# Copying the half tile's weights on the sync engine, one quarter in each of four rounds

## The chip, the cores and the metric

The kernel runs on one core of one Trainium2 chip. The metric is the device time of one execution in microseconds. The engines are PE (TensorE, matrix products), DVE (VectorE), ACT (ScalarE), POOL (GpSimd) and SP (SyncE, which here only issues DMAs). A difference of over 0.3% (about 1.1 us) is what a measurement of this kernel can tell from none.

## What is computed

A gated block: a LayerNorm and a cross-attention of 2048 tokens (8 sequences of 256, width 256) over 77 context rows each, then a LayerNorm and a feed-forward part. The feed-forward part has a shared expert for all tokens and two routed experts, each token going to one of them. Cut to what matters:

```
def ffn(x):                                   # x: 2048 tokens, width 256
    top1 = argmax(softmax(x @ gate_w.T))      # 0 or 1 for each token
    masked = x[None] * one_hot(top1).T[:, :, None]
    h = relu(einsum('end,edh->enh', masked, w1) + b1[:, None])    # hidden width 1024
    routed = (einsum('enh,ehd->end', h, w2) + b2[:, None]).sum(0)
    return routed + relu(x @ sw1 + sb1) @ sw2 + sb2

x = x + tanh(g_xattn) * xattn(layernorm(x), ctx)
x = x + tanh(g_ffn) * ffn(layernorm(x))
```

For the expert that a token is not sent to, the masked row is zero, so that expert gives a constant row, relu(b1) @ w2, which the kernel works out once from its weights (the tile `other_sum`).

## The kernel before

Every matrix product runs on float32 data that is cut into a high and a low part (`_hi`, `_lo`), in three products: high by high, high by low, low by high. ACT makes the high part out of a PSUM bank, DVE or GpSimd subtracts it to get the low part. So each step of PE has one of ACT and one of DVE (or GpSimd) behind it before PE can use the result.

**The first stage** (0 to about 226 us) holds the attention of eight batches and the shared expert's feed-forward part in five units. Its order is written out by hand, an order for each engine (`PE_ORDER`, `ACT_ORDER`, `DVE_ORDER`, `POOL_ORDER`, `SP_ORDER`); a word such as `tn.5.0.1` is a step, its indices and, last, which of two PSUM banks (`bank`) it uses. The steps that matter here:
- `sc.b.k` on PE: scores of batch b, quarter k; then `sm` and `ss` on DVE (maxima L1246, the shift L1258), `ex` on ACT, `su` on DVE (sums L1264 and reciprocals L1268), `di` on GpSimd (the division L678);
- `tn` transposes of the probabilities (L1668), `va` the product with the values and `val` its low part on DVE (L1273), `ou` the output product, `x1` the addition to x (L1282);
- `xn2` on ACT (L964) and `n2` on PE (L1705): second LayerNorm and its transposes; `h` and `y`: the shared expert's two products; `hl` (L1379) the low part of h;
- `ot.e.part` on DVE (L1228, L1232): half of the sums over `w2` for `other_sum` of expert e, four instructions each; `ch` (L1302 and on): which expert a token goes to; `scat` on GpSimd: the scatter of the tokens' rows into `sorted_dram`, sorted by expert.

**The seam.** When the last counts are there, DVE writes a plan of five integers to SBUF (`plan_int`): how many tiles of 256 sorted rows belong to the first expert (`first`), how many rounds there are (`rounds`, eight on this data), whether a tile is taken twice, and place and expert of a half tile that both experts share. Each engine loads those that it needs into registers with `value_load` (L576 to L579 on SP, L782 and L783 on GpSimd, L1062 to L1064 on ACT, L1462 and L1463 on DVE). SP does that after it has issued the store of the last unit of the shared part (L545, `ps.4`), which waits for DVE's addition (L1388).

**The routed stage** is a loop of eight rounds on every engine. Round j multiplies one tile of 256 sorted rows with one expert's weights, which lie in SBUF in `ew`. PE makes eight chunks of h (four banks, so three run ahead), from the fourth on a chunk of y after each (L1535), and behind the seventh chunk of h, ahead of the fourth of y, it transposes the tile of the round to come, `sorted_turn(j + 1)`, L1772; for that the tile must have been loaded into `xs`. SP loads it (L549) once the tile before has been transposed and once DVE has copied that one's token numbers (`ids_copied`, L1475), which DVE does right after its first low part of the round:

```
with sp.Fori(0, rounds - 1) as j:
    sp.wait_ge(xsT_ps, j + 1)
    sp.wait_ge(ids_copied, j + 1)
    load_sorted(j + 1 - again)
```

GpSimd gathers the rows of `part_dram` (what the shared expert gave) with two indirect DMAs (L795), adds the constant row (L802), waits for DVE's `final` (L1488, which takes y and part), and scatters it to `out` (L808).

**The half tile** comes last (from about 331 us). Its expert is known at the seam only, so its weights are copied from `ew` over the shared expert's, which are free when the shared part is done. ACT issues those four copies of 1 MB each, before its loop (L1071, L1074); PE waits for them with `half_w` just before the half tile:

```
act.wait_ge(y_used, CHUNKS_SHARED)
for n in range(2, 6):
    act.wait_ge(w_lo[n], 1)
for n in range(2):
    act.dma_start(sw1_sb[n]..., ew[:, bass.ds(half_expert, 1), n, :]...).then_inc(half_w, 16)
    act.dma_start(sw2_sb[n]..., ew[:, bass.ds(half_expert, 1), 2 + n, :]...).then_inc(half_w, 16)
```

## Time and profile before

| | |
|---|---|
| three runs | 352.29, 352.46, 353.43 us; median 352.46 |
| the profiled execution's own time | 350.86 us |
| its span | 349.1 us |
| PE busy | 319.1 us (91% of the span) |
| DVE, ACT, POOL busy | 230.1, 216.4, 184.4 us |
| TensorE's granted clock, mean | 0.974 of full |
| moved by DMA | 35.69 MB |

The span is the time from the first to the last instruction that the profile holds; the execution's own time has 1.8 us more around it. The profile gives the busy time of each engine in all, and in stretches; which wait ended an engine's idle time; and a chain of waits, followed back from the last instruction. Times of instructions are counted from the span's start. The granted clock is 1.00 at 2.4 GHz and 0.50 at 1.2 GHz.

### The profile page before, as it was taken

How to read it: one execution, taken by the hardware profiler on the slowest of the kernel's cores; microseconds unless marked ns; L12 is line 12 of the kernel's file. 1: busy time of each engine (PE TensorE's matmuls, PEld its weight loads, DVE VectorE, ACT ScalarE, POOL GpSimd, SP SyncE). 2: the span in 40 equal slices, each digit the busy share in tenths (PEclk: the TensorE clock that was granted, in tenths of full speed). 3: DMA queues.
4: the chain of work that ended last, by engine and by line, in shares of the span. 5: the costliest groups of instructions: out<-in, count | busy, mean ns of one | idle time of the engine just before them, and what ended most of it. 6: DMA issues, size and time to landing. Idle time of an engine off the chain costs nothing.

```text
span 349.1 us, 7274 instructions
## 1 busy us (share of the span) xinstructions
PE 319.1 (91%) x2363; PEld 284.6 (82%) x2363; DVE 230.1 (66%) x516; ACT 216.4 (62%) x483; POOL 184.4 (53%) x261
## 2 busy tenths in 40 slices
PE   7996688999989999999999999964999999999980
PEld 7764557779878788887998899964999999999970
DVE  6999789899989878877847936321344454445370
ACT  2765998869577577579764854442447554755560
POOL 8317989893643485736530775303245434563441
PEclk9999899999999999999999999988999999999995
DMA  6991846636131040431421004095023212321310
GB/s 192 297 327 31 257 103 157 141 95 207 16 94 38 5 118 0 107 105 48 168 74 60 0 17 141 29 366 207 4 86 90 67 25 88 92 60 30 91 46 12
DMA packets 38151, 35.69 MB, mean 102 GB/s; under 512 B 16608, under 2 KB 35060, under 8 KB 37613
## 3 DMA queue, kind: packets, MB, share of 16 engines
q1 hardware_dynamic: 33992, 23.17, 24.2%
q0 software_dynamic: 2720, 7.32, 6.4%
q10 hardware_dynamic: 1413, 4.87, 3.8%
q8 instruction: 14, 0.23, 0.3%
q14 instruction: 12, 0.10, 0.1%
HBM read 21.20 MB, written 9.85 MB: 89 GB/s over the span
## 4 chain that ended last, share of the span: by engine, by line
PE 68%; DVE 11%; DMA 7%; ACT 6%; issue 3%; SPq 2%; POOL 0%; ACTq 0%; DVEq 0%; POOLq 0%
PE y_ps L1535 25%; PE h_ps L1535 18%; PE bank L1535 10%; PE s_ps L1535 9%; DMA x_all<-in_x 5%; PE bank L1668 4%; DMA xs<-sorted_dram 3%; DVE rsum L1264 1%; PE bank L1772 1%; DVE stats L1147 1%; DVE probs L1258 1%; ACT xn L885 1%; DVE smax L1246 1%; PE bank L1705 1%; ACT pT L943 1%
## 5 line engine op out<-in xcount | busy, mean ns | idle before, releaser
L678 POOL TENSOR_TENSOR probs<-probs,rinv 128x616 f32<-128x616 f32 x32 | 41.3, 1294 | 37.2 <-DVE rinv L1268 36.9
L1469 DVE TENSOR_TENSOR hT_lo<-h,hT_hi 128x256 fp32r<-128x256 f32 x64 | 29.6, 463 | 43.4 <-ACT h L1086 43.4
L1535 PE MATMUL y_ps<-ew,hT_hi 128*128 128x256 f32 x256 | 54.3, 290 | 3.0 <-DVE hT_lo L1469 3.0
L1535 PEld LDWEIGHTS y_ps<-ew,hT_hi 128*128 128x128 f32 x256 | 43.4, 194 | 3.2 <-DVE hT_lo L1469 3.2
L1535 PE MATMUL y_ps<-sw_hi,hT_hi 128*128 128x256 f32 x136 | 40.7, 299 | 1.2 <-DVE hT_lo L1513 1.2
L982 ACT ACTIVATE hT_hi<-h_ps,vec_cols 128x512 fp32r<-128x512 f32 (+1 forms) x40 | 24.3, 608 | 24.0 <-PE h_ps L1535 23.6
L1535 PE MATMUL y_ps<-sw_lo,hT_hi 128*128 128x256 f32 x136 | 38.4, 282 | 0.0
L1535 PE MATMUL y_ps<-sw_hi,hT_lo 128*128 128x256 f32 x136 | 38.4, 282 | 0.0
L1083 ACT ACTIVATE hT_hi<-h_ps,vec_cols 128x256 fp32r<-128x256 f32 x32 | 15.2, 475 | 35.1 <-PE h_ps L1535 28.5
L1535 PE MATMUL y_ps<-ew,hT_lo 128*128 128x256 f32 x128 | 36.6, 286 | 0.0
L808 POOL DMA_INDIRECT out<-final,scatter_token x16 | 18.1, 1129 | 30.2 <-issue 30.2
L1264 DVE TENSOR_REDUCE rsum<-probs 128x8 f32<-128x616 f32 x32 | 25.1, 786 | 9.7 <-ACT probs L934 4.8
L1535 PE MATMUL h_ps<-x2T_hi,sw_hi 128*128 128x512 f32 (+1 forms) x80 | 29.7, 371 | 0.0
L704 POOL TENSOR_TENSOR hT_lo<-h,hT_hi 128x512 fp32r<-128x512 f32 (+1 forms) x15 | 17.3, 1156 | 23.0 <-ACT h L987 22.8
L1535 PEld LDWEIGHTS y_ps<-sw_hi,hT_hi 128*128 128x128 f32 x136 | 25.9, 191 | 2.8 <-DVE hT_lo L1513 1.8
L1535 PE MATMUL h_ps<-x2T_hi,sw_lo 128*128 128x512 f32 (+1 forms) x80 | 27.9, 349 | 0.0
L1535 PE MATMUL h_ps<-x2T_lo,sw_hi 128*128 128x512 f32 (+1 forms) x80 | 27.8, 348 | 0.0
L943 ACT ACTIVATE pT<-bank 128x512 f32<-128x512 f32 x40 | 23.4, 604 | 6.8 <-PE bank L1668 6.6
L1379 DVE TENSOR_TENSOR hT_lo<-h,hT_hi 128x512 fp32r<-128x512 f32 (+1 forms) x25 | 17.5, 701 | 15.3 <-ACT h L987 15.2
L1535 PE MATMUL h_ps<-xsT_parts,ew 128*128 x192 | 27.0, 284 | 0.0
L1535 PE MATMUL s_ps<-xsT_parts,ew 128*128 x192 | 26.9, 283 | 0.0
L1535 PEld LDWEIGHTS y_ps<-sw_hi,hT_lo 128*128 128x128 f32 x136 | 25.9, 191 | 0.2
(214 smaller groups left out, 920.1 us busy)
## 6 DMA issues: line engine op xcount, KB each, us to landing
v_diag<-v_rows SPq DMA_DIRECT2D x16, 256.0 KB
stage<-in_L_ffn_w SPq DMA_DIRECT2D x4, 1024.0 KB, 5.7
xs<-sorted_dram SPq DMA_DIRECT2D x8, 257.0 KB
stage<-in_L_ffn_sw SPq DMA_DIRECT2D x2, 1024.0 KB, 6.7
sw_hi<-ew ACTq DMA_DIRECT2D x2, 1024.0 KB, 5.9
sw_lo<-ew ACTq DMA_DIRECT2D x2, 1024.0 KB, 10.2
x_all<-in_x SPq DMA_DIRECT2D x1, 1536.0 KB, 10.1
part_dram<-x_all SPq DMA_DIRECT2D x3, 512.0 KB, 2.9
```

What stands on the lines that cost most here:

```text
L678: nc.gpsimd.tensor_tensor(pq, pq, rinv[:, b % 2, k, :].unsqueeze(2).to_broadcast([P, HG, KEYS]), ALU.mult).then_inc(p_ready, 1)
L704: nc.gpsimd.tensor_tensor(hT[1][:, q % HB, 0:width], h32[:, q % 2, 0:width], hT[0][:, q % HB, 0:width], ALU.subtract).then_inc(h_lo_pool, 1)
L808: pool.indirect_dma_start(out=out[:, :], out_offset=bass.IndirectOffsetOnAxis(ap=scatter_token[:, t:t + 1], axis=0), in_=final[:, t, :], i ...
L885: ins = nc.scalar.activation(xn[:, b % 2, t, :], x_all[:, n, :], ACT.Identity, scale=rstd[:, n:n + 1], bias=shift[:, n:n + 1])
L943: nc.scalar.activation(pT[:, 2 * u:2 * u + 2, :].rearrange("p c s -> p (c s)"), bank[m][:, :], ACT.Copy).then_inc(pT_sb, 1)
L982: nc.scalar.activation(hT[0][:, q % HB, 0:width], h_ps[:, q % 2, 0:width], ACT.Relu, bias=b1_sb[:, 0, c:c + 1]).then_inc(h_hi, 1)
L1083: nc.scalar.activation(hT[0][:, c % HB, 0:RTOK], hidden_bank(c % 4)[:, 0:RTOK], ACT.Relu, bias=b1_sb[:, 1 + e, c:c + 1]).then_inc(h_hi, 1)
L1264: nc.vector.tensor_reduce(out=rsum[:, b % 2, k, :], in_=probs[:, b % 2, k, :].rearrange("p (h k) -> p h k", k=KEYS), axis=AX_X, op=ALU.add ...
L1379: nc.vector.tensor_tensor(hT[1][:, q % HB, 0:width], h32[:, q % 2, 0:width], hT[0][:, q % HB, 0:width], ALU.subtract).then_inc(h_lo, 1)
L1469: nc.vector.tensor_tensor(hT[1][:, c % HB, 0:RTOK], h32[:, c % 2, 0:RTOK], hT[0][:, c % HB, 0:RTOK], ALU.subtract).then_inc(h_lo, 1)
L1535: return nc.tensor.matmul(out_, lhsT, rhs, start=start, stop=stop, **kw)
L1668: ins = nc.tensor.transpose(bank[m][0:ROWS[c], v * SEQ + t * P:v * SEQ + (t + 1) * P], probs[:, b % 2, g * TB + t, ROW0[c]:ROW0[c] + ROWS[ ...
```

## The change

There are four edits.

1. ACT no longer issues the four copies, and no longer loads `half_expert`. SP issues them, one in each of its rounds 0 to 3, right behind that round's load of a tile, on the same queue. So that a register can choose the quarter, the shared expert's four weight tiles become one tile `sw` with an index of four.
2. SP waits once for the experts' low parts (`w_lo`) ahead of its loop, and its loop is cut in two, rounds 0 to 3 and the rest.
3. GpSimd drains once in every round (`pool.drain()`), behind its two additions and ahead of its wait for `final_rdy`.
4. The written orders of the first stage change. Up to the middle of the stage only DVE, ACT and GpSimd differ; from batch 5 on many steps use the other of the two banks (the routed stage too: `SORTED_BANK` 0), and a few steps change places. Two of the lines that show it, the second a cut row of `PE_ORDER`:

```
-SORTED_BANK = 1
+SORTED_BANK = 0
-    y.1.2 sc.6.1 tn.5.0.1 ou.4.0 h.1.6 tn.5.1.1 y.1.3 sc.6.2 h.1.7 tn.5.2.0
+    y.1.2 tn.5.0.0 ou.4.1 h.1.6 sc.6.1 tn.5.1.0 y.1.3 h.1.7 tn.5.2.1 sc.6.2
```

The rest of the diff:

```
-        sw1_sb = [sb(f"sw1_{n}", [P, KC, HIDDEN], F32R) for n in ("hi", "lo")]
-        sw2_sb = [sb(f"sw2_{n}", [P, HC, DIM], F32R) for n in ("hi", "lo")]
+        sw = sb("sw", [P, 4, KC * HIDDEN], F32R)
+        sw1_sb = [sw[:, n, :].rearrange("p (k h) -> p k h", k=KC) for n in range(2)]
+        sw2_sb = [sw[:, 2 + n, :].rearrange("p (k d) -> p k d", k=HC) for n in range(2)]
...
-            with sp.Fori(0, rounds - 1) as j:
+            def routed(j):
                 sp.wait_ge(xsT_ps, j + 1)
                 sp.wait_ge(ids_copied, j + 1)
                 load_sorted(j + 1 - again)
+
+
+            for n in range(2, 6):
+                sp.wait_ge(w_lo[n], 1)
+            with sp.Fori(0, 4) as j:
+                routed(j)
+                sp.wait_ge(y_used, CHUNKS_SHARED)
+                sp.dma_start(sw[:, bass.ds(j, 1), :].rearrange("p o h -> p (o h)").bitcast(F32),
+                             ew[:, bass.ds(half_expert, 1), bass.ds(j, 1), :].rearrange("p e o h -> p (e o h)").bitcast(F32)
+                             ).then_inc(half_w, 16)
+            with sp.Fori(4, rounds - 1) as j:
+                routed(j)
...
                     nc.gpsimd.tensor_tensor(part[:, t, :], part[:, t, :], other_row[:, 1 - e, :], ALU.add
                                             ).then_inc(part_rdy, 1)
+                pool.drain()
                 pool.wait_ge(seam_rdy, 1)
...
-            half_expert = act.value_load(plan_int[0:1, HALF_EXPERT:HALF_EXPERT + 1], min_val=0, max_val=1)
-
-
-            act.wait_ge(y_used, CHUNKS_SHARED)
-            for n in range(2, 6):
-                act.wait_ge(w_lo[n], 1)
-            for n in range(2):
-                act.dma_start(sw1_sb[n][:, :, :].rearrange("p k h -> p (k h)").bitcast(F32),
-                              ew[:, bass.ds(half_expert, 1), n, :].rearrange("p o h -> p (o h)").bitcast(F32)
-                              ).then_inc(half_w, 16)
-                act.dma_start(sw2_sb[n][:, :, :].rearrange("p k d -> p (k d)").bitcast(F32),
-                              ew[:, bass.ds(half_expert, 1), 2 + n, :].rearrange("p o h -> p (o h)").bitcast(F32)
-                              ).then_inc(half_w, 16)
```

**SP at the head of the routed loop** (`xs<-sorted_dram` is a tile's load, `sw<-ew` a copy of 1 MB, `ISA` a register operation that carries waits). Before:

```order
L579 ISA x2
L581 UNCONDITIONAL_BRANCH
L581 ISA
L549 ISA
L549 DMA xs<-sorted_dram 128x2x257
L581 ISA
L581 COMPARE_AND_BRANCH
```

and now (from L589 on the changed kernel's line numbers):

```order
L579 ISA x2
L589 UNCONDITIONAL_BRANCH
L589 ISA
L549 ISA
L549 DMA xs<-sorted_dram 128x2x257
L592 ISA
L592 REGISTER_ALU
L592 DMA sw<-ew 128x2048
L589 REGISTER_ALU
L589 COMPARE_AND_BRANCH
```

The load keeps its place as the first DMA of SP's loop, and the copy stands behind it.

**ACT at the head of the routed loop.** Before:

```order
L1064 TENSOR_LOAD plan_int
L1064 ISA x2
L1071 ISA
L1071 DMA sw_hi<-ew 128x2048
L1074 ISA
L1074 DMA sw_hi<-ew 128x2048
L1071 ISA
L1071 DMA sw_lo<-ew 128x2048
L1074 ISA
L1074 DMA sw_lo<-ew 128x2048
L1095 UNCONDITIONAL_BRANCH
```

and now (its L1076 is the L1063 of before):

```order
L1076 TENSOR_LOAD plan_int
L1076 ISA x2
L1095 UNCONDITIONAL_BRANCH
L1095 ISA
L1082 REGISTER_ALU
L1083 ACTIVATE hT_hi<-h_ps,vec_cols 128x256
```

The loop's first ACTIVATE now comes right behind the two register loads.

**DVE around the shift of batch 5's last scores** (`ss.5.3` is the first L1258 here). Before:

```order
L1258 TENSOR_TENSOR probs<-s_ps,smax 128x616
L1273 TENSOR_TENSOR oT_lo<-bank,oT_hi 128x512
L1264 TENSOR_REDUCE rsum<-probs 128x8
L1268 RECIPROCAL rinv<-rsum 128x8
L1246 TENSOR_REDUCE smax<-s_ps 128x8
L1258 TENSOR_TENSOR probs<-s_ps,smax 128x616
```

and now:

```order
L1258 TENSOR_TENSOR probs<-s_ps,smax 128x616
L1228 TENSOR_SCALAR other_sum<-stage,relu_b 128x256
L1232 SCALAR_TENSOR_TENSOR other_sum<-stage,relu_b,other_sum 128x256 x3
L1273 TENSOR_TENSOR oT_lo<-bank,oT_hi 128x512
L1232 SCALAR_TENSOR_TENSOR other_sum<-stage,relu_b,other_sum 128x256 x4
L1264 TENSOR_REDUCE rsum<-probs 128x8
L1268 RECIPROCAL rinv<-rsum 128x8
```

The eight instructions of `ot.0.0` and `ot.0.1` stood some 45 us earlier, between 79 and 93 us of the profile, and stand here now.

## Rows read from the trace of the kernel before

**Rows 1.** Busy time by stretch: stretch and its length, engines, clock, DMA share, GB/s
```profile
120.00:160.00 40.00, 40.00 (x295) 33.89 (x292) 31.66 (x79) 26.36 (x61) 25.85 (x36) 1.00 0.28 80
220.00:240.00 20.00, 15.23 (x113) 14.70 (x111) 6.17 (x13) 8.45 (x21) 4.80 (x6) 0.91 0.62 238
240.00:260.00 20.00, 17.30 (x135) 17.30 (x136) 6.66 (x14) 8.32 (x20) 7.30 (x8) 0.91 0.18 52
280.00:300.00 20.00, 20.00 (x172) 20.00 (x171) 9.57 (x21) 11.77 (x30) 9.15 (x10) 1.00 0.20 48
```

**Rows 2.** The chain of waits, 226 to 262 us: start, length, what
```profile
226.44 0.76 DVE x_all L1388
...
227.69 1.09 SPq L576
...
233.08 9.58 DMA xs<-sorted_dram
...
251.90 0.71 PE y_ps L1535 x6
...
256.13 0.44 PE bank L1772 x4
```

**Rows 3.** The timeline around the first round: start, length, instruction, idle before it
```profile
226.53 0.57 ACTq L1071 DMA_DIRECT2D sw_hi<-ew  x1
...
230.85 0.47 ACT L1083 ACTIVATE hT_hi<-h_ps,vec_cols 128x256 fp32r<-128x256 f32 x1 [6.57 <-issue]
...
232.20 0.48 PE L1535 MATMUL y_ps<-ew,hT_hi 128*128 128x256 f32 x1 [2.99 <-DVE hT_lo L1469]
...
242.70 1.11 PE L1772 MATMUL bank<-ident,xs 128*128 128x128 f32 x4 [4.48 <-DMA xs<-sorted_dram]
```

**Rows 4.** Busy time in three short stretches, columns as in rows 1
```profile
233.00:234.00 1.00, 1.00 (x7) 1.00 (x7) 0.52 (x2) 0.88 (x3) 0.00 (x0) 0.50 1.05 434
240.00:241.00 1.00, 0.00 (x0) 0.00 (x0) 0.00 (x0) 0.00 (x0) 0.00 (x0) 1.00 0.64 240
242.70:246.00 3.30, 3.30 (x16) 3.30 (x17) 0.69 (x1) 0.60 (x1) 1.41 (x2) 0.50 0.00 0
```

**Rows 5.** DMA from 216.9 to 223 us in 40 slices, and SP's issue
```profile
GB/s 369 329 363 282 67 0 27 161 88 135 243 310 351 250 148 41 7 7 20 20 27 0 0 0 0 0 0 0 0 0 0 0 0 0 0 0 0 0 0 0
...
216.92 0.37 SPq L549 DMA_DIRECT2D xs<-sorted_dram  x1
```

**Rows 6.** The timeline of PE: two transposes that it waited for
```profile
98.84 0.63 PE L1705 MATMUL bank<-ident,xn 128*128 128x128 f32 x4 [0.75 <-ACT xn L964]
...
100.59 0.66 PE L1705 MATMUL bank<-ident,xn 128*128 128x128 f32 x4 [0.41 <-DVE oT_lo L1273]
```

**Rows 7.** The timeline of DVE: the sums that move, and a wait near their new place
```profile
79.19 0.35 DVE L1228 TENSOR_SCALAR other_sum<-stage,relu_b 128x256 f32<-128x256 f32 x1
79.58 1.89 DVE L1232 SCALAR_TENSOR_TENSOR other_sum<-stage,relu_b,other_sum 128x256 f32<-128x256 f32 x3
...
90.64 2.04 DVE L1232 SCALAR_TENSOR_TENSOR other_sum<-stage,relu_b,other_sum 128x256 f32<-128x256 f32 x4
...
128.30 0.79 DVE L1264 TENSOR_REDUCE rsum<-probs 128x8 f32<-128x616 f32 x1 [1.55 <-ACT probs L924]
```

**Rows 8.** The timeline of GpSimd, and DVE's two sums of a round
```profile
235.88 1.07 POOL L795 DMA_INDIRECT part<-part_dram,gather_token  x1 [11.73 <-issue]
...
243.32 1.41 POOL L802 TENSOR_TENSOR part<-part,other_row 128x256 f32<-128x256 f32 x2 [5.07 <-DMA part<-part_dram,gather_token]
...
253.85 1.04 POOL L795 DMA_INDIRECT part<-part_dram,gather_token  x1 [0.30 <-issue]
...
258.09 1.43 POOL L802 TENSOR_TENSOR part<-part,other_row 128x256 f32<-128x256 f32 x2 [1.87 <-DMA part<-part_dram,gather_token]
...
249.29 0.75 DVE L1488 SCALAR_TENSOR_TENSOR final<-y_ps,gains,part 128x512 f32<-128x512 f32 x1 [1.69 <-PE y_ps L1535]
...
261.03 0.75 DVE L1488 SCALAR_TENSOR_TENSOR final<-y_ps,gains,part 128x512 f32<-128x512 f32 x1 [1.23 <-PE y_ps L1535]
```

53 lines of the change are left out of this document (26 added, 27 removed).

## The prediction

> **What bounds the kernel now.** I read three views, in this order. The busy time by stretch shows where PE rests: over 120 to 160 us and over 280 to 300 us it is busy throughout, so the late first stage and the steady rounds are PE's, but of 220 to 240 us it works 15.23, and of 240 to 260 us 17.30, at a clock of 0.91 [rows 1]. That is the step from the first stage into the routed one. The chain of waits says what these 7.5 us wait for: DVE's last addition of the shared part, then SP, which from 227.69 us on loads its four registers at about 1.1 us each, then one DMA, the load of tile 1, from 233.08 to 242.66 us, then PE's transposes at 242.70, which waited 4.48 us for it [rows 2, 3]. The timeline gives the rest: ACT issues four copies from 226.53 us on and starts the routed part only at 230.85, after 6.57 us; PE gets its first low part at 232.20, after 2.99 us of idle time [rows 3]. After both rests the clock stands at 0.50: in the stretch at 233 us and in that from 242.70 us on [rows 4].
>
> The load takes 9.58 us because it shares the DMA engines with 4 MB of copies: at 233 us they are fully busy (share 1.05, 434 GB/s), and only at 240 us does that fall to 0.64 [rows 4]. The same instruction for tile 0 was issued at 216.92 us, with no copy beside it, and the last bytes move in the 21st slice of 0.1525 us, so within 3.2 us [rows 5].
>
> **Part by part.**
>
> *ACT issues nothing.* PE has its four banks of h filled at 229.21 (232.20 less 2.99 [rows 3]); at 0.71 us a chunk [rows 2] the first was there at about 227.1, and ACT can start then. DVE has its own two register loads to do behind the addition that ends at 227.20; at SP's 1.09 us each [rows 2] it is ready by 229.4 at the latest. So PE's first y starts at 229.2 to 229.9 instead of 232.20, and the 2.99 us go. But what is late next is the load: PE's work from the first y to the transposes is 4.23 us in the next round (251.90 to 256.13 [rows 2]), so it stands at the transposes at 233.4 to 234.1 and waits there. Worth nothing by itself: the load hides it.
>
> *The load without copies beside it.* SP's own chain does not get shorter; the four waits on `w_lo` were fulfilled long ago and cost a few hundredths each (estimate: 0.1 us, from the pieces around the load that are not 1 us long). Issue at 233.2, 3.1 us for the transfer (the last slices of rows 5 carry next to nothing, and PE needs the completion), so 236.3 us instead of 242.66: **6.4 us** less. Bounds on the transfer: not under 2.5 us (the bulk in rows 5 is over after 16 slices), not over some 4.6 us (in the round after, SP may issue the load only once the first low part is made, PE's first y begins right behind that at 251.90, and PE transposes at 256.13 without waiting [rows 2]).
>
> *The copies.* Each goes behind its round's load on SP's queue, is 1 MB, and takes about 3.3 us of all engines (four of them, from about 227.5 to 240.6 us [rows 3, 4]) in a round of 11.74 us (249.29 to 261.03 [rows 8]). The next load is issued a round later, so it finds the queue empty. PE needs the copies only behind its eighth round; the last is issued in round 3. The gathers of `part` do meet the copy: alone they take 4.24 us from the first issue to the additions (253.85 to 258.09), among the four copies 7.44 (235.88 to 243.32 [rows 8]). With one copy, which began before them, I expect about 1 us more, and the cover is this: the additions end at 259.52, `final` waits for PE until 261.03, so 1.2 us are free in each round (with 0.3 us between them), and PE needs `final` only with the first y of the next round, 1.9 us after it ends (250.04 to 251.90). Cost 0.
>
> *The drain.* It stands behind additions that are over at 259.52 and ahead of a wait that ends at 261.78. The trace has no drain on GpSimd that I could read; it costs between 0 and, as a bound from the nearest GpSimd instructions, the 1.43 us of the two additions [rows 8]. I take what is left of their running time, which is hidden: 0. Uncovered it would delay only the scatter.
>
> *The orders of the first stage.* The eight `ot` instructions leave DVE's stretch from 79 to 93 us, 0.35 + 1.89 + 2.04 us [rows 7]. Behind that stretch PE waits twice, 0.75 us for ACT's `xn2` and 0.41 us for DVE's low part [rows 6]; `xn2` now stands ahead of one shared chunk on ACT, and DVE is earlier. At most 1.16 us go; I take **0.8**. At 123 us the same 4.3 us come in ahead of and behind `val.4`; DVE has 1.55 us of idle time before 128.30 [rows 7], and `sc.6.1` and `sc.6.2` on PE, which wait for the scores before them to be read, were moved behind other steps of PE (a transpose, an output product and an h chunk; an h chunk and a transpose), which is what such a lateness needs. I take 0 there. The changed banks are the same work in the other bank.
>
> *The clock.* PE will still rest 2.2 to 2.8 us before the transposes (236.3 less 233.4 to 234.1). Both rests at the seam, 2.99 and 4.48 us [rows 3], were followed by a stretch at 0.50, the second by 3.3 us of it on the path (242.70 to 246.00 [rows 4]). I expect one again: 0. If none comes, half of 3.3 us, 1.6 us, is gained.
>
> The sum: 6.4 + 0.8 = 7.2 us. The profiled execution took 350.86 us (span 349.1), so it would take 343.7; it lies 1.6 us below the median of the three runs, 352.46, to which the same is applied: **345.3 us**.
>
> One rule of the Trainium skill speaks against the plain reading. "DMA: Bandwidth & Descriptors", section "Issuing engines are not separate DMA queues", says that DMAs of any engine run on the same 16 DMA engines and interleave, and that spreading the issue saves only sequencer time. The trace agrees on the sharing; on the sequencer it shows 6.57 us of idle ACT for four issues and two register loads, which is not small. By that rule alone the copy behind the load would still eat into it; that is the first rival.
>
> **The rivals.**
>
> 1. *The copy slows its own load.* The copy can be issued some 0.4 us after the load (the issue's own 0.37 us [rows 5]), which needs 3.1 us. If they share the engines evenly, the load ends up to one copy later, 3.3 us. For it: the load of tile 1 was slowed by exactly such copies. Against: there they were on another queue and ahead. It would also reach into rounds 1 to 3, where the load has 4.6 us at most. Time: 345.3 + 3.3 = 348.6.
> 2. *DVE is late at 123 us.* The 4.3 us of sums against 1.55 us idle: 2.7 us stand on PE's path if the moved score steps do not cover them, and PE has no rest of its own there (120 to 160 us [rows 1]). Time: 348.0.
> 3. *GpSimd's loop becomes the bound, and the kernel slower.* If each gather among copies takes 3.2 us more, as in round 0 (7.44 less 4.24), four rounds are 2.0 us late each, less 1.9 us of PE's slack: 6.1 us. A drain of length X delays the scatter by X less 1.05 us (the time in which `final` is made) in each of them. Above X = 1.3 us the gain is gone; at 2.4 us (as long as both scatters' issues) it is 6.1 + 4 x 1.35 + 4 x 0.15 = 12.1 us against 7.2: 357.4. Against: the adds are 1.4 us in all, and only one copy is there at a time.
> 4. *The load is slow by itself* in the loop's first round and the copies only lie beside it. Then only 0.8 us go: 351.7. Rows 5 speak against it.
>
> **How the numbers follow.** Forecast 0.79, rivals 0.08, 0.07, 0.04, 0.02. The range: at the low end the clock's 1.6 us and the rest of the 1.16 us, 343.3, rounded to 343.0 for the transfer's lower bound; at the high end the first rival, 348.5. Faster by over 0.3% (under 351.4; about what a measurement can tell): forecast and rivals 1 and 2, 0.94; within it rival 4, 0.02; slower rival 3, 0.04.
>
> **What would show it.** The chain of waits should hold SP's register loads, then the load of about 3 us and the transposes near 236; ACT's first routed ACTIVATE near 227.1; no idle PE before the first y, or under 0.8 us; PE waiting 2 to 3 us for `xs` once, then 0.50 for 3.4 us. PE's waits at 98.8 and 100.6 should be gone or smaller, and none new between 122 and 137. Rounds of 11.74 us throughout, the additions of rounds 0 to 3 up to 1 us later. I am wrong if the load takes over 4.6 us, if PE waits for `final`, or if DVE's last addition of the shared part starts later than at 226.44.

## The result, and the profile after

| | before | changed |
|---|---|---|
| runs | 351.59 to 353.43 us, median 352.38 (4) | 339.61 to 343.43 us, median 340.71 (4) |
| the profiled execution | 350.86 us, span 349.1 | 340.90 us, span 339.1 |
| PE busy | 319.1 us | 318.2 us |
| TensorE's granted clock, mean | 0.974 | 0.980 |

The ratio is 0.9679 with a 95% interval of 0.9616 to 0.9741. The medians lie 11.7 us apart, and the interval stands for 9.1 to 13.5 us. The forecast was 7.1 us faster (345.3 us), its range ended at 343.0. The direction was right and the size was not: 4.6 us more came than was forecast.

The busy time by stretch of the changed kernel, beside [rows 1] (same columns):

```profile
120.00:160.00 40.00, 38.69 (x286) 32.41 (x283) 34.76 (x83) 24.31 (x54) 25.15 (x35) 1.00 0.28 80
220.00:240.00 20.00, 19.63 (x165) 19.29 (x164) 7.66 (x16) 10.48 (x26) 5.26 (x6) 1.00 0.33 106
240.00:260.00 20.00, 19.39 (x160) 18.77 (x159) 7.75 (x19) 10.97 (x27) 11.34 (x12) 1.00 0.45 150
280.00:300.00 20.00, 20.00 (x172) 20.00 (x171) 8.86 (x21) 12.11 (x31) 11.30 (x12) 1.00 0.27 79
```

PE works 19.63 us of 220 to 240 us, where it was 15.23, and the clock is full at the seam, where it was 0.91. Between 120 and 160 us it now has 1.3 us of gaps that it did not have.

The timeline of the changed kernel around the first round (start, length, instruction, idle before it), beside [rows 3]:

```profile
227.57 0.75 DVE L1388 SCALAR_TENSOR_TENSOR x_all<-y_ps,gains,x_all 128x512 f32<-128x512 f32 x1 [1.07 <-PE y_ps L1535]
228.36 0.48 ACT L1083 ACTIVATE hT_hi<-h_ps,vec_cols 128x256 fp32r<-128x256 f32 x1 [2.96 <-PE h_ps L1535]
232.01 0.42 SPq L549 DMA_DIRECT2D xs<-sorted_dram  x1
232.78 0.63 SPq L592 DMA_DIRECT2D sw<-ew  x1
234.93 0.66 PE L1772 MATMUL bank<-ident,xs 128*128 128x128 f32 x4 [0.37 <-DMA xs<-sorted_dram]
```

ACT starts the routed part 0.79 us behind the start of DVE's addition (it was 4.41), the load is issued 4.44 us behind it (it was 6.64), and PE waits 0.37 us for `xs` where it waited 4.48. PE has no wait of its own before its first y. The last two rows put a bound on the load: issued at 232.01 and used at 234.93, at most 2.9 us, where the forecast had 3.1 and the kernel before 9.58 [rows 2].

SP's four register loads, by source line (duration in ns min/median/max, then the start), which I had priced at 1.09 us each whatever happens:

```profile
L576 SPq TENSOR_LOAD <-plan_int x1: 607/607/607, 228.8 to 228.8; - x1
L577 SPq TENSOR_LOAD <-plan_int x1: 282/282/282, 229.8 to 229.8; - x1
L578 SPq TENSOR_LOAD <-plan_int x1: 262/262/262, 230.3 to 230.3; - x1
L579 SPq TENSOR_LOAD <-plan_int x1: 273/273/273, 230.9 to 230.9; - x1
```

Together they take 1.42 us, where the chain of before has 1.09 us for the first alone [rows 2] and the four together take 3.77.

The end of the program, which I had not read at all: GpSimd's last instruction but for its semaphores is a drain, the instruction that the third edit adds to every round. This one belongs to the end of the block (L177). Before and after:

```profile
L177 POOLq DRAIN  x1: 4650/4650/4650, 344.2 to 344.2; - x1
```

```profile
L177 POOLq DRAIN  x1: 375/375/375, 338.5 to 338.5; - x1
```

And DVE's last sum of the loop and that of the half tile (L1488, L1528), in the timelines of before and of the changed kernel:

```profile
331.57 0.75 DVE L1488 SCALAR_TENSOR_TENSOR final<-y_ps,gains,part 128x512 f32<-128x512 f32 x1 [1.53 <-PE y_ps L1535]
340.34 0.48 DVE L1528 SCALAR_TENSOR_TENSOR half_final<-y_ps,gains,half_part 128x256 f32<-128x256 f32 x1 [0.80 <-PE y_ps L1535]
```

```profile
325.78 0.75 DVE L1488 SCALAR_TENSOR_TENSOR final<-y_ps,gains,part 128x512 f32<-128x512 f32 x1 [1.24 <-PE y_ps L1535]
334.60 0.48 DVE L1528 SCALAR_TENSOR_TENSOR half_final<-y_ps,gains,half_part 128x256 f32<-128x256 f32 x1 [0.80 <-PE y_ps L1535]
```

With these milestones the 10.0 us between the two spans can be laid out, each line the difference of two starts:

| stretch | before | changed | less |
|---|---|---|---|
| start to DVE's last shared addition | 226.44 | 227.57 | -1.13 |
| from there to the first transposes of the loop (242.70, 234.93) | 16.26 | 7.36 | 8.90 |
| to the first `final` (249.29, 241.86) | 6.59 | 6.93 | -0.34 |
| to the eighth `final` (331.57, 325.78) | 82.28 | 83.92 | -1.64 |
| to the half tile's (340.34, 334.60) | 8.77 | 8.82 | -0.05 |
| to the end of the span | 8.8 | 4.5 | 4.3 |

So the seam gave 8.9 us, the end 4.3, and 3.2 us were given back, in the first stage and in the rounds. The profiled execution of before lies 1.5 us under its median, that of the changed kernel 0.2 us over its own; the rest of the 11.7 us is in that. Two theories had to be told apart for each: for the end, that the drains in the rounds shorten it (A) or that something in the copies' move does (B); for the seam, that the bytes of the copies slow three different things (register loads, ACT's own issues, the load), or that the issues as such do.

### The profile page after: what moved, and what is told of

Its sections match the earlier page's. It is cut to its first block, busy times and chain, and to the rows that moved or that the text cites. A ratio compares the mean times of both kernels' runs of the same rounds, so it can differ in the third digit from the quotient of the medians.

```text
span 339.1 us, 7286 instructions
## 1 busy us (share of the span) xinstructions
PE 318.2 (94%) x2363; PEld 282.2 (83%) x2363; DVE 227.9 (67%) x516; ACT 215.6 (64%) x483; POOL 184.0 (54%) x261
## 4 chain that ended last, share of the span: by engine, by line
PE 61%; DVE 15%; ACT 8%; issue 7%; DMA 5%; POOL 1%; POOLq 1%; SPq 1%; DVEq 0%; ACTq 0%
PE y_ps L1535 20%; PE h_ps L1535 17%; PE bank L1535 9%; PE s_ps L1535 9%; DMA x_all<-in_x 5%; PE bank L1668 4%; ACT probs L947 2%; DVE rsum L1264 2%; DVE smax L1246 1%; DVE probs L1258 1%; DVE stats L1147 1%; DVE other_sum L1232 1%; ACT pT L956 1%; DVE hT_lo L1469 1%; ACT xn L898 1%
## 5 line engine op out<-in xcount | busy, mean ns | idle before, releaser
L690 POOL TENSOR_TENSOR probs<-probs,rinv 128x616 f32<-128x616 f32 x32 | 39.1, 1223 | 37.8 <-DVE rinv L1268 37.5
L1535 PE MATMUL y_ps<-sw,hT_hi 128*128 128x256 f32 x272 | 57.1, 290 | 1.2 <-DVE hT_lo L1513 1.2
L1535 PEld LDWEIGHTS y_ps<-sw,hT_hi 128*128 128x128 f32 x272 | 44.9, 191 | 2.9 <-DVE hT_lo L1513 1.8
L1535 PE MATMUL h_ps<-x2T_hi,sw 128*128 128x512 f32 (+1 forms) x160 | 43.6, 359 | 0.1
L1535 PE MATMUL y_ps<-sw,hT_lo 128*128 128x256 f32 x136 | 38.4, 282 | 0.0
L1535 PEld LDWEIGHTS h_ps<-x2T_hi,sw 128*128 128x128 f32 x160 | 26.8, 190 | 3.5 <-issue 0.8
L1535 PE MATMUL h_ps<-x2T_lo,sw 128*128 128x512 f32 (+1 forms) x80 | 27.8, 348 | 0.0
L1379 DVE TENSOR_TENSOR hT_lo<-h,hT_hi 128x512 fp32r<-128x512 f32 (+1 forms) x25 | 16.2, 654 | 15.0 <-ACT h L1000 15.0
L1535 PEld LDWEIGHTS y_ps<-sw,hT_lo 128*128 128x128 f32 x136 | 26.0, 191 | 0.2
L1668 PE MATMUL bank<-ident,probs 128*128 128x128 f32 (+1 forms) x160 | 24.3, 284 | 1.4 <-ACT pT L956 1.0
```

The costliest lines, as they stand in the source:

```text
L690: nc.gpsimd.tensor_tensor(pq, pq, rinv[:, b % 2, k, :].unsqueeze(2).to_broadcast([P, HG, KEYS]), ALU.mult).then_inc(p_ready, 1)
L1379: nc.vector.tensor_tensor(hT[1][:, q % HB, 0:width], h32[:, q % 2, 0:width], hT[0][:, q % HB, 0:width], ALU.subtract).then_inc(h_lo, 1)
L1535: return nc.tensor.matmul(out_, lhsT, rhs, start=start, stop=stop, **kw)
L1668: ins = nc.tensor.transpose(bank[m][0:ROWS[c], v * SEQ + t * P:v * SEQ + (t + 1) * P], probs[:, b % 2, g * TB + t, ROW0[c]:ROW0[c] + ROWS[ ...
```

## The experiments

Each kernel was timed beside the kernel before on the same chip (its own runs and those of before stand beside each other; the chips differ by some us, so medians are compared within a row or a table only). The intervals are 0.4 to 0.6% wide to each side, so what is under 2 us is read from the traces and not from the times. Diffs are cut to what changes.

### Which part of the change gives what: e1, e2, e3, e5

The changed kernel without the drain (e1), and the kernel before with the drain (e2):

```
-                pool.drain()
                 pool.wait_ge(seam_rdy, 1)
```

```
                                             ).then_inc(part_rdy, 1)
+                pool.drain()
                 pool.wait_ge(seam_rdy, 1)
```

> The changed kernel without GpSimd's drain in the rounds; all else as changed. Theory A (the trace of the changed kernel): the drain that GpSimd makes at the very end of the program took 4.65 us before and 0.38 us now, because the drains in the rounds have left it nothing to do, so the tail grows again by 4.3 us: 345.0 us. If the drains are also what makes three rounds longer (periods of 12.1 to 12.6 us among 11.75), that comes back and it is 342.6 us with periods of 11.75. Theory B (the drain does nothing, the end is shorter since the copies left ACT's queue): 340.7 us, tail unchanged. The prediction's own price, 0, says 340.7 us too.

> The kernel before with the drain in each round as the one edit. Theory A: the seam stays, the tail loses 4.3 us: 352.4 - 4.3 = 348.1 us; if the drains lengthen some rounds by 0.8 us, up to 350.5. Theory B and the prediction's price of 0: 352.4 us, with about 9.2 us between PE's last product and the end as before.

e3 is the changed kernel without the drain and with `SORTED_BANK` and all written orders of before; e5 is the kernel before with `SORTED_BANK` and all written orders of the change:

> The copies on SP, a quarter in each of rounds 0 to 3, with the orders of before and no drain. The prediction's term: 6.4 us, so 346.0 us, with register loads on SP of 1 us each and PE resting 2 to 3 us before the transposes. Theory A: the register loads were slowed by the copies too and take 0.3 us each, PE rests under 1 us, both stretches at half clock go: 2.99 + 4.48 + 3.3 = 10.8 us, so 341.6 us; with rounds lengthened by the copies 344.0 us. Theory B (the tail too comes from this edit): 337.3 us.

> The new orders and banks alone in the kernel before. The prediction's term: 0.8 us less, 351.6 us, with DVE's last shared addition at 225.6. Reading of the two traces: PE's waits at 98.8 and 100.6 us go (1.9 us less at 105 us), and new ones come between 122 and 150 us (1.5 to 2 us): 352.0 to 352.7 us. If the bank of the routed stage's transposes lengthens rounds (ACT late by 1.5 us once a round): 354 to 355 us.

| kernel | median (range) | before beside it | ratio (95%) |
|---|---|---|---|
| e1, changed without drain | 344.52 (342.81 to 347.93) | 349.77 | 0.9854 (0.9799 to 0.9910) |
| e2, drain alone | 345.35 (342.70 to 346.42) | 349.77 | 0.9855 (0.9806 to 0.9904) |
| e3, copies on SP alone | 346.19 (343.87 to 347.65) | 349.77 | 0.9872 (0.9822 to 0.9921) |
| e5, orders alone | 350.23 (347.52 to 352.34) | 349.77 | 1.0014 (0.9973 to 1.0054) |

The drain by itself gives 4.4 us by the medians (3.4 to 6.8 by the interval), as theory A said (4.3). The last drain of the program, in e1 and in e2:

```profile
L177 POOLq DRAIN  x1: 4650/4650/4650, 336.2 to 336.2; - x1
```

```profile
L177 POOLq DRAIN  x1: 375/375/375, 340.4 to 340.4; - x1
```

Theory B falls: e1 has the copies on SP and its end takes 4.65 us all the same. e2's rounds stayed between 11.72 and 11.94 us, so drains do not lengthen them. The orders by themselves give nothing that can be measured; my 0.8 us (a ratio of 0.998) lies inside the interval, and so does 0. e3 gave 3.6 us, less than any of the numbers that stood ready for it (6.4, 8.4 and 10.8). In its trace the seam is as short as in the changed kernel, the shared addition at 229.82 us and the transposes at 236.92, so 7.10 us; but the addition came 3.4 us later than in the kernel before, and its rounds took 83.7 us where those of before took 82.3. With six runs over 3.8 us, and the interval up to 0.9921, how much this edit is worth alone stays open between 2.8 and 6.2 us. e1, which has it and the orders, gave 5.25 (3.1 to 7.0).

The traces of this chip say why that is less than the 8.9 us of the first pair. Two of them have the copies on ACT, e2 and e5, and from the shared addition to the transposes they take 14.42 and 14.70 us, not 16.26, since PE rests only 1.35 and 2.83 us for `xs`. The seam of e1 and e3 (7.16 and 7.10) is then 7.4 us shorter. And the first two turns of the loop, from the first transposes to the third, take 25.99 and 26.21 us in e1 and e3, and 23.55 and 23.56 in e2 and e5. What is left is about 5 us, which is e1's gain and lies within e3's interval.

### Both kernels again on one chip, and the shape of the copies: e6 to e9

> The kernel before once more, profiled on the chip that runs the next three. If the load of tile 1 took 9.6 us because of the four copies alone, it takes 9.6 again, and PE rests 4.5 us at the transposes. In the kernels with parts of the change that left the copies on ACT (the drain alone, the orders alone) it took 7.7 and 8.0 us and PE rested 1.35 and 2.83 us: if that is how much one execution differs from another, this trace shows 7.5 to 9.6 us, and the seam of the first trace was a slow one. ACT's stalls of 1.0 to 1.5 us ahead of one ACTIVATE a round, which the first trace lacked and the other five have: present here too if they belong to single executions, absent if the edits bring them.

> The changed kernel once more on the same chip. If the parts add up (on the other chip: drain alone -4.4 us, copies alone -3.6, the drain taken from the whole +4 from the sum of what is left), it is 8 to 10 us faster than before here; if the 11.7 us of the first comparison hold everywhere, 11.7.

e8 takes the drain out of the rounds and puts one behind the loop:

```
                 routed(j, 1)
 
+            pool.drain()
             pool.wait_ge(half_ids, 1)
```

> The changed kernel with one drain of GpSimd behind its loop, ahead of the half tile, in place of one a round. Theory A, form 1 (the drain at the end works off what has piled up since the last drain): the one drain takes some 4 us, beside the half tile's wait, where GpSimd has about 3 us to spare ahead of its gather; the drain at the end is 0.4 us, and the time that of the changed kernel to +1 us. Form 2 (the drain at the end is long if any DMA of GpSimd was issued since the last one): in the changed kernel there are four such DMAs behind the last drain and it took 0.38 us, so form 2 is already unlikely; it would give +4.3 us here and there alike.

e9 issues all four copies behind the first load of the loop:

```
-            with sp.Fori(0, 4) as j:
+            with sp.Fori(0, 1) as j:
                 routed(j)
-                sp.wait_ge(y_used, CHUNKS_SHARED)
-                sp.dma_start(sw[:, bass.ds(j, 1), :]..., ew[:, bass.ds(half_expert, 1), bass.ds(j, 1), :]...)
-            with sp.Fori(4, rounds - 1) as j:
+            sp.wait_ge(y_used, CHUNKS_SHARED)
+            for n in range(4):
+                sp.dma_start(sw[:, n:n + 1, :]..., ew[:, bass.ds(half_expert, 1), n:n + 1, :]...)
+            with sp.Fori(1, rounds - 1) as j:
```

> The changed kernel, but all four copies behind SP's first load of the loop, back to back. If what helps is only that the load of tile 1 and the register loads come ahead of the copies, the first turn is as in the changed kernel (PE waits under 1 us for xs); the gathers of rounds 0 and 1 then share with 13 us of copies, and the second load stands behind them on the queue: PE waits for part or xs once, 1 to 4 us: +1 to +4 us. If the quarters cost nothing and neither do four at once: +0.

| kernel | median (range) | before beside it | ratio (95%) |
|---|---|---|---|
| e6, before again | 350.09 (348.57 to 353.08) | 351.12 | 0.9979 (0.9943 to 1.0015) |
| e7, changed again | 341.06 (337.50 to 343.58) | 351.12 | 0.9752 (0.9703 to 0.9801) |
| e8, one drain behind the loop | 343.41 (343.20 to 345.27) | 351.12 | 0.9811 (0.9765 to 0.9856) |
| e9, four copies behind the first load | 342.51 (341.20 to 344.50) | 351.12 | 0.9772 (0.9724 to 0.9820) |

On this chip the change is worth 8.7 us by the ratio (7 to 10.4). The first comparison gave more, but the two intervals overlap, so a difference between them is not shown. The seam of before repeats: in e6's timeline

```profile
234.12 0.58 PE L1535 MATMUL y_ps<-ew,hT_hi 128*128 128x256 f32 x1 [2.98 <-DVE hT_lo L1469]
244.48 1.12 PE L1772 MATMUL bank<-ident,xs 128*128 128x128 f32 x4 [4.43 <-DMA xs<-sorted_dram]
```

stand the same two rests as in [rows 3], 2.98 and 4.43 us, and e7's has one of 0.26 us at 233.27. From the shared addition (228.38, 226.02) to the transposes it is 16.10 us against 7.25. So two traces of the kernel before have 16.1 to 16.3 us, and the two of e2 and e5, with the same copies, 14.4 to 14.7. Whether that is the chip or the execution was not tested; the seam is worth 7.3 to 8.9 us by these.

e8 shows what the long drain is. In its profile, by source line, the one drain behind the loop and the one at the end, and in GpSimd's timeline the work around it:

```profile
L830 POOLq DRAIN  x1: 6427/6427/6427, 326.2 to 326.2; - x1
```

```profile
L177 POOLq DRAIN  x1: 217/217/217, 341.1 to 341.1; - x1
```

```profile
327.08 1.00 POOL L820 DMA_INDIRECT out<-final,scatter_token  x1 [0.30 <-issue]
333.33 1.04 POOL L832 DMA_INDIRECT half_part<-part_dram,half_token  x1 [5.25 <-issue]
```

The drain starts at 326.15, finds the last scatters still to be issued, and is over at 332.58 (326.15 + 6.43), 4.5 us behind the last one's issue (327.08 + 1.00). Of the 5.25 us that GpSimd is idle before the half tile's gather the changed kernel has 0.30, and the sum of the half tile waits for that gather: it starts 12.94 us behind the eighth `final`, against 8.82. So the price is not saved, only moved to where it is on the path. The median, 343.41 us, is 2.4 us behind that of the changed kernel, and the intervals just overlap; the 4.1 us are read from the trace. Theory A holds in its first form, and my estimate of 3 us to spare was too high.

e9 shows what the quartering is for. The first transposes are as in the changed kernel (PE waited 0.33 us for `xs`), the copies' place behind the load is what helps there; but the gather of round 0 then stands in 4 MB of copies:

```profile
243.94 1.40 POOL L815 TENSOR_TENSOR part<-part,other_row 128x256 f32<-128x256 f32 x2 [8.23 <-DMA part<-part_dram,gather_token]
246.50 0.39 PE L1536 MATMUL y_ps<-ew,hT_hi 128*128 128x256 f32 x1 [3.63 <-DVE hT_lo L1470]
```

GpSimd waits 8.23 us for it, and PE 3.63 us for a low part that DVE could make only behind `final`. From the first transposes to the next PE takes 15.69 us, where the changed kernel takes 12.13 here (e7). The median is 1.5 us longer, which the intervals do not tell from none.

### What the bytes do, and what a copy costs in a round: e10 to e13

e10 is the kernel before with the same four issues on ACT, of 64 bytes a partition each instead of 8 KB (its half tile is computed with the shared expert's weights but for these):

```
-                act.dma_start(sw1_sb[n][:, :, :]..., ew[:, bass.ds(half_expert, 1), n, :]...)
+                act.dma_start(sw1_sb[n][:, 0, 0:16]..., ew[:, bass.ds(half_expert, 1), n, 0:16]...)
...
-                act.dma_start(sw2_sb[n][:, :, :]..., ew[:, bass.ds(half_expert, 1), 2 + n, :]...)
+                act.dma_start(sw2_sb[n][:, 0, 0:16]..., ew[:, bass.ds(half_expert, 1), 2 + n, 0:16]...)
```

> The kernel before with ACT's four issues in their place, but each copies only the first 16 of 2048 numbers of a partition (64 bytes): the issues stay, the bytes go. The half tile is computed with the shared expert's weights and so is not the reference's. Theory A1 (the bytes slow the register loads and the load): SP's register loads fall from 1.07, 0.91, 0.94, 0.90 us to 0.6, 0.3, 0.3, 0.3, the load is issued 2 us earlier and takes 3 to 4 us, PE waits less than 1 us at the transposes. ACT's wait is the test of the issues: if an issue costs ACT's queue 0.5 to 1.3 us whatever it copies, PE still rests about 3 us before its first y, and the gain is the 4.4 us of the second rest with its slow stretch of 1.7: 350.1 - 6.1 = 344.0 us. If the later two issues (1.3 us each) were slow because of the bytes, PE rests about 1.5 us: 342.5. The prediction's split (register loads 1.1 us each whatever is copied): load issued at 233, first turn 2 to 3 us later than A1: 346 us.

e11 leaves out the copies of the changed kernel and PE's wait for them (its half tile is computed with the shared expert's weights):

```
             with sp.Fori(0, 4) as j:
                 routed(j)
-                sp.wait_ge(y_used, CHUNKS_SHARED)
-                sp.dma_start(sw[:, bass.ds(j, 1), :]..., ew[...]...).then_inc(half_w, 16)
...
-            pe.wait_ge(half_w, 16 * 4)
```

> The changed kernel without its four copies and without the wait for them (the half tile is computed with the shared expert's weights, so it is not the reference's). The prediction's price of the copies, 0: 341.1 us as the changed kernel. If the copies lengthen the gathers of rounds 0 to 3, the one of round 0 falls from 7.0 to 7.4 us (first gather to additions) to 4.3, and DVE's first final is no longer late: -0.5 to -1 us. Rival (the copies are what lengthens rounds 1 to 3 to 12.0 to 12.6 us): -2 us and periods of 11.75 throughout.

e12 makes the copies in rounds 1 to 4, with `j - 1` as the quarter; e13 is the changed kernel with `SORTED_BANK` and all orders of before:

```
-            with sp.Fori(0, 4) as j:
+            with sp.Fori(0, 1) as j:
+                routed(j)
+            with sp.Fori(1, 5) as j:
                 routed(j)
```

> The changed kernel with the four copies in rounds 1 to 4 in place of 0 to 3, so that the seam's first gather (which stands behind the last store of the shared part) has none beside it. If the copy is what makes it 7 us, it takes 4.3 to 5 here, PE's waits of 0.3 to 0.9 us behind the first final go, and it is 0.3 to 1 us faster than the changed kernel; if the gather is slow for another reason (the store, or the first of its kind), +0.

> The changed kernel with the orders and banks of before. The prediction's term: the orders are worth 0.8 us, so 341.9 us. The orders alone gave 1.0014 (0.9973 to 1.0054) of before, so between -0.5 and +1.5 us is expected here: 340.6 to 342.6 us, with DVE's last shared addition at 225.6 to 228.4 as in the kernels with the old orders so far.

| kernel | median (range) | before beside it | ratio (95%) |
|---|---|---|---|
| e10, small copies on ACT | 345.47 (343.51 to 347.89) | 352.41 | 0.9813 (0.9762 to 0.9865) |
| e11, changed without copies | 339.77 (338.61 to 343.35) | 352.41 | 0.9667 (0.9613 to 0.9720) |
| e12, copies in rounds 1 to 4 | 342.29 (340.50 to 344.78) | 352.41 | 0.9715 (0.9669 to 0.9761) |
| e13, changed with old orders | 342.04 (341.29 to 345.00) | 352.41 | 0.9731 (0.9683 to 0.9779) |

e10's queues and PE around the seam, by source line and in the timelines of ACT and PE. First SP's register loads, then ACT's last two issues, then PE:

```profile
L576 SPq TENSOR_LOAD <-plan_int x1: 605/605/605, 230.1 to 230.1; - x1
L577 SPq TENSOR_LOAD <-plan_int x1: 309/309/309, 231.0 to 231.0; - x1
L578 SPq TENSOR_LOAD <-plan_int x1: 267/267/267, 231.6 to 231.6; - x1
L579 SPq TENSOR_LOAD <-plan_int x1: 274/274/274, 232.2 to 232.2; - x1
```

```profile
230.22 0.55 ACTq L1071 DMA_DIRECT2D sw_lo<-ew  x1
230.88 0.55 ACTq L1074 DMA_DIRECT2D sw_lo<-ew  x1
233.07 0.38 PE L1535 MATMUL y_ps<-ew,hT_hi 128*128 128x256 f32 x1 [1.50 <-DVE hT_lo L1469]
237.41 0.60 PE L1772 MATMUL bank<-ident,xs 128*128 128x128 f32 x4
```

and the same register loads of the kernel before, in e6:

```profile
L576 SPq TENSOR_LOAD <-plan_int x1: 1068/1068/1068, 229.6 to 229.6; - x1
L577 SPq TENSOR_LOAD <-plan_int x1: 913/913/913, 231.0 to 231.0; - x1
L578 SPq TENSOR_LOAD <-plan_int x1: 936/936/936, 232.2 to 232.2; - x1
L579 SPq TENSOR_LOAD <-plan_int x1: 895/895/895, 233.5 to 233.5; - x1
```

With the issues in place and the bytes gone, the register loads take 1.46 us in all instead of 3.81; ACT's third and fourth issue 0.55 us instead of the 1.3 they took with their bytes; PE rests 1.50 us before its first y instead of 2.98, and not at all at the transposes, which come 8.60 us behind the shared addition (228.81), against 16.1 before and 7.25 to 7.4 in the changed kernel. So of the 8.8 us of the seam the bytes made 7.5 and the issues the other 1.3 (5.8 and 1.3 if the 14.4 us of e2 are taken for the seam with its bytes). Theory A1 had this right, with PE's rest of 1.5 us in its second form, which forecast 7.6 us less than before; the median is 6.9 us less than that of before beside it, and the interval 4.8 to 8.4.

The price of a copy in a round, in GpSimd's timelines of the changed kernel, of e11 and of e12, round 0 (the additions behind the gather; the gather's first issue was at 233.05, 233.13 and 237.37):

```profile
240.40 1.42 POOL L814 TENSOR_TENSOR part<-part,other_row 128x256 f32<-128x256 f32 x2 [4.97 <-DMA part<-part_dram,gather_token]
241.86 0.75 DVE L1488 SCALAR_TENSOR_TENSOR final<-y_ps,gains,part 128x512 f32<-128x512 f32 x1 [3.52 <-POOL part L814]
```

```profile
237.54 1.61 POOL L810 TENSOR_TENSOR part<-part,other_row 128x256 f32<-128x256 f32 x2 [2.02 <-DMA part<-part_dram,gather_token]
```

```profile
241.50 1.61 POOL L816 TENSOR_TENSOR part<-part,other_row 128x256 f32<-128x256 f32 x2 [1.75 <-DMA part<-part_dram,gather_token]
```

From issue to additions it is 7.35 us beside one copy, and 4.41 and 4.13 us without: here one copy lengthens the gather by 3 us, not by the 1 us of my forecast, and DVE's first `final` waits 3.52 us for it. That holds in round 0, where the copy is issued 0.27 us before the gather (232.78 and 233.05). In rounds 1 and 2 it is issued 3.4 and 1.6 us before the gather, which takes 4.26 and 5.12 us (5.24 in round 3), against 4.21 to 4.28 in the same rounds of before: 0 to 1 us more, as forecast.

PE feels round 0's gather by how late it is. From the first transposes to the next PE takes 11.74 to 11.82 us in e10, e11 and e12, which have no copy of 1 MB beside that gather (5.35, 4.41 and 4.13 us). With one copy it takes 11.82 us where the gather took 5.96 (e8), 12.13 at 6.95 (e7), 12.40 at 7.35 (the changed kernel), 12.73 at 7.60 (e16), 13.11 at 7.77 (e3), and 15.69 beside four (10.62, e9). So in the first turn a copy costs 0 to 1.3 us, 0.6 in the changed kernel. Its second turn takes 12.62 us where e10 has 11.73; but e11, without any copy, has 12.49, and what makes that turn long stays open. The times show none of this: e12, moved to repair the first gather, is not faster than the changed kernel by its ratio. e13 agrees with e5 that the orders are worth little: its ratio, 0.9731, lies between the changed kernel's 0.9638 and 0.9752 on other chips.

### What the long drain consists of: e14 to e16

e14 has one drain ahead of the loop, where GpSimd waits for the last store anyway, and none in the rounds; e15 drains only in the rounds of the second expert:

```
             pool.wait_ge(other_rdy, 1)
+            pool.drain()
...
-                pool.drain()
```

```
-                pool.drain()
+                if e == 1:
+                    pool.drain()
```

> The changed kernel with one drain of GpSimd ahead of its loop (behind the memset and the constant row's sum, where it waits for the last store of the shared part anyway) and none in the rounds. In the changed kernel the drain of round 0 ended 2.1 us behind the additions and the later ones 0.4 to 0.5 us, and the single drain behind the loop took until 4.5 us behind the last scatter. Theory P (a drain works off what the indirect DMAs since the last drain have left, about 0.1 us for each, an estimate from these: 18 DMAs for 2.1 us, 50 for 4.65): the drain at the end has the 34 DMAs of the routed stage and takes 2.6 to 3.4 us, the tail is 7.2 to 7.9 us (4.9 as changed, 9.2 without drains): changed + 2.7 us. Rival Q (the long drain is a fixed 4.6 us once there was any loop since the last one): tail 9.2 us, changed + 4.3 us.

> The changed kernel with the drain only in the rounds of the second expert. Theory P: the first of these drains ends 3 to 4 us behind its additions (18 DMAs of the first stage and 16 of four rounds, an estimate of 0.1 us each), which delays one scatter by 1 to 2 us and nothing on PE's path; the drain at the end is 0.38 us and the time that of the changed kernel. Rival (the drains of the early rounds are what makes rounds longer): 1 to 2 us less than the changed kernel.

> The changed kernel a third time, as the measure for the two above on their chip: 340 to 342 us, a tail of 4.92 us. Its rounds are 11.75 us where ACT is not late at the fifth chunk of h, and 12.1 to 12.9 where it starts that chunk over 1.2 us behind PE.

| kernel | median (range) | before beside it | ratio (95%) |
|---|---|---|---|
| e14, one drain ahead of the loop | 340.09 (338.23 to 340.43) | 348.92 | 0.9708 (0.9659 to 0.9757) |
| e15, drains for the second expert | 337.36 (335.43 to 342.31) | 348.92 | 0.9641 (0.9587 to 0.9695) |
| e16, changed again | 337.40 (336.04 to 341.24) | 348.92 | 0.9638 (0.9590 to 0.9685) |

The drain at the end of e14, by source line, and the three drains that e15's trace holds for its rounds:

```profile
L177 POOLq DRAIN  x1: 2835/2835/2835, 335.6 to 335.6; - x1
```

```profile
L817 POOLq DRAIN  x3: 1865/2055/5168, 300.2 to 324.2; - x3
```

e14's last drain takes 2.84 us: neither 0.4 nor 4.65. Its median is 2.7 us above e16's, the number that theory P gave; the intervals overlap, so the trace decides (2.46 us more than the 0.38 of the others). (On this data the second expert has the last three rounds, not four as I wrote.) The first drain in e15, which has the first stage and five rounds to work off, takes 5.17 us, of which 1.5 are the additions in front of it; it ends 3.7 us behind them, and the round after it takes 12.24 us instead of 11.75, which the median does not show: the time is that of the changed kernel. The profiled executions of e15 and e16 were 4 to 5 us longer than their medians, by a late first stage, so only what stands behind the shared addition is read from them. So a drain of GpSimd costs by the DMAs that it has issued since the last one (rival Q falls), it is free where GpSimd waits anyway, and the early drains lengthen nothing.

The expectations counted indirect DMAs alone, and by that count the price of one is not the same everywhere (2.84 us for 34, 4.65 for 50). GpSimd issues six plain loads too, at the start of the program. e14's first drain, which stands behind all of the first stage's, settles which count holds:

```profile
L792 POOLq DRAIN  x1: 1867/1867/1867, 224.6 to 224.6; - x1
```

It has 16 indirect and 6 plain DMAs to account for. Counted like this, the drains that have no work in front of them are 0.22 us for 2 DMAs (e8's last), 0.38 for 4 (the changed kernel's), 1.87 for 22, 2.84 for 34 and 4.65 for 56 (before): 0.05 us and 0.082 us for each, to within 0.02 us. The same line gives, to within 0.04 us, how long those behind additions or scatters take beyond them: 2.06 us for 24 (round 0), 0.40 for 4, 3.69 for 44 (e15's first) and 4.50 for 54 (e8). The plain ones moved 0.5 to 256 KB each, so it goes by their number and not by their bytes; nor does it go by the time since the last drain, which was 224 us for the 1.87 and about 110 us for the 2.84. What GpSimd does for each in a drain no trace shows.

## Why the prediction missed

**The drain.** I wrote: "Uncovered it would delay only the scatter", cost 0, and its only other role was in rival 3, as a loss. The cost was right: the drains in the rounds end 0.4 us behind the additions and lie in the wait for `final` (in round 0 it is 2.1 us, and this one ends 1.3 us behind `final`, which delays a scatter alone); e15 and e2 show no price. What failed is that the sum had no line for the end of the program. The end of the span stood 8.8 us behind the last sum, and the scatter in between takes 1.02 us to issue and about 2.4 to land; the 4.65 us that were left over were an instruction of the very kind that the change adds. This is the largest term that I missed, 4.3 us.

The misses do not simply add up to the 4.6 us. In the two profiled executions I forecast 343.7 and 340.9 was measured, 2.8 us less: 4.3 us at the end and 2.5 at the seam came on top, and 1.9 us in the first stage and 2.0 us behind the first transposes, which I had not forecast either, went the other way. The other 1.8 us lie between these executions and the medians. That the total came within 5 us is partly luck.

**The register loads.** The step "SP's own chain does not get shorter" was wrong. I took 1.09 us as what a load of a register costs; it was what it costs beside 4 MB of copies. e10 gives 0.61 us for the first and about 0.28 for the next ones once the bytes are gone. The load was issued 4.44 us behind the addition and not 6.64, 2.2 us sooner. The Trainium skill has a floor of 600 ns for such a load ("DMA: Bandwidth & Descriptors", section "Latency and other measured facts"); SP's first load bears it out (0.61 us), the next ones lie at half of it, so here the trace decides and it is no floor. Weighed in the forecast, even that floor would have said that 1.09 us has something in it.

**ACT and the clock.** "Worth nothing by itself: the load hides it" holds for a load at 236.3; with the load at 234.9 nothing was left for it to hide, PE's rests went from 2.99 and 4.48 us to 0 and 0.37, and no stretch at 0.50 followed. I had expected one again, and had the 1.6 us of it as the low end only. The size was right: the turn behind the slow start took 13.26 us in the kernel before and takes 11.74 at full clock in e10. But the late gather took 0.6 us of it back in the first turn. Of ACT's 6.57 us before its first routed ACTIVATE, which I put down to four issues and two register loads, 2.96 are there without any issue: so long ACT waits for PE's first chunk in the changed kernel. The transfer itself was as forecast (at most 2.9 us against 3.1), and the first rival fell: the copy issued 0.77 us behind the load did not slow it beyond the forecast. The rule of the Trainium skill on shared DMA engines ("DMA: Bandwidth & Descriptors", "Issuing engines are not separate DMA queues") stands with this addition from the trace: an issue takes 0.55 us on ACT's sequencer, and 1.3 us when 2 MB are in flight before it, so the time that it calls usually small grew to 3.7 us for four.

In the seam the forecast was 6.4 us and the traces show 8.9 and 8.85. In the first pair 2.0 us were lost again between the transposes and the half tile's sum, in e6 and e7 nothing was. Without the end of the program the spans differ by 5.7 us in the first pair and by 11.4 in e6 and e7, with 3.5 us of difference in the first stage between the two pairs: my 7.2 us lie among these.

**The rounds.** "Rounds of 11.74 us throughout" holds for few traces. The seven periods behind the first `final` take 82.3 us in the first trace of before, 83.9 in that of the changed kernel, and 81.5 to 85.5 in the others. It is not the copies (e11 has none and 84.8 us), not the drains (e10 has none and 83.3) and not the orders (e13 has those of before and 85.0). In most rounds that take over 12 us ACT starts the fifth chunk's high part long after PE has made it. The round of 12.54 us in ACT's and DVE's timelines of the changed kernel, and the same chunk in that of before:

```profile
301.45 0.75 DVE L1488 SCALAR_TENSOR_TENSOR final<-y_ps,gains,part 128x512 f32<-128x512 f32 x1 [1.26 <-PE y_ps L1535]
307.36 0.47 ACT L1083 ACTIVATE hT_hi<-h_ps,vec_cols 128x256 fp32r<-128x256 f32 x1 [2.23 <-PE h_ps L1535]
313.99 0.75 DVE L1488 SCALAR_TENSOR_TENSOR final<-y_ps,gains,part 128x512 f32<-128x512 f32 x1 [1.23 <-PE y_ps L1535]
```

```profile
312.13 0.47 ACT L1083 ACTIVATE hT_hi<-h_ps,vec_cols 128x256 fp32r<-128x256 f32 x1 [0.43 <-PE h_ps L1535]
```

2.23 us idle instead of 0.43, and nothing that the trace shows holds it: PE's chunk was made at 305.5. This occurs in most rounds of thirteen of the seventeen traces, e6 of the kernel before among them, and in none of the first trace of before nor of e14, e15 and e16, which ran on one chip. So it does not come from the change; whether it belongs to the chip was not tested, and what it is stays open. Where the same change is timed with it and without it, it is worth 0.9752 (e7) and 0.9638 (e16), on chips that may differ in more than this.

**The first stage.** I expected 0.8 us less and said that I would be wrong if the last shared addition came later than at 226.44; it came at 227.57. The waits at 98.8 and 100.6 us [rows 6] did go, and PE is busy 40.00 us of 80 to 120 us, where it was 38.83:

```profile
80.00:120.00 40.00, 38.83 (x293) 33.31 (x294) 35.66 (x76) 28.17 (x65) 18.36 (x28) 1.00 0.30 76
```

```profile
80.00:120.00 40.00, 40.00 (x306) 34.56 (x307) 33.52 (x73) 29.69 (x68) 18.82 (x29) 1.00 0.30 77
```

But my second rival came in a small size. PE's timeline of the changed kernel has

```profile
131.21 0.41 PE L1535 MATMUL s_ps<-k_own,q_hi 64*128 64x308 f32 x2 [0.65 <-DVE probs L1258]
```

behind DVE's eight sums; PE's busy time in 120 to 160 us fell by 1.3 [rows 1]. This goes with the orders in all seventeen traces: 40.00 us and 38.6 to 38.7 in the eleven with the new ones, 38.8 and 40.00 in the six with the old. So the orders move 1.2 us of PE's rest from one place to the other, and my 0.8 us were gained and lost again. And the clock fell early in one trace longer than in the other. The stretch from 30 to 44 us of before, of the changed kernel, and of e7:

```profile
30.00:44.00 14.00, 9.82 (x65) 7.60 (x65) 11.71 (x20) 12.43 (x34) 12.47 (x20) 0.88 0.65 174
```

```profile
30.00:44.00 14.00, 11.02 (x60) 8.82 (x59) 10.98 (x19) 11.82 (x32) 11.74 (x19) 0.63 0.69 175
```

```profile
30.00:44.00 14.00, 9.37 (x68) 6.87 (x69) 11.89 (x20) 12.97 (x35) 12.61 (x21) 1.00 0.71 187
```

These are 0.88, 0.63 and 1.00 of full clock. The last shared addition stood between 225.6 and 229.8 us in the traces with the old orders and between 226.0 and 231.9 in those with the new. The four latest (e3, e12, e15, e16) were already behind at 20 us: their traces hold 82 or 83 matrix products of PE up to there, and that of the kernel before 97; why is open. A gain of 0.8 us can't be read in this, and the timings (e5, e13) can't tell it from none.

**The copies.** I priced them at 0, with "about 1 us more" for the gather and a copy "which began before them". In rounds 1 to 3 that is what came (0 to 1 us). In round 0 the copy and the gather start together, the gather took 3 us more, and the cover that I named (1.2 us free, then 1.9 us of PE's slack) was used up. PE then waited 0.33 us for a low part that DVE makes behind `final`, so this sign of being wrong came true; the turn was 0.6 us longer.

**The other rivals.** GpSimd did not become the bound (rival 3): a slow gather held `final` up for long in round 0 alone (3.52 us; in round 1 0.1 us more than where PE is what it waits for). The load was not slow by itself (rival 4).

**The range.** Its low end had the clock and the rest of the orders, but no unknown that could pay: every mechanism that I had not read was placed on the slow side.
